# Folding the token numbers into the lower one-hots on VectorE, and moving the upper one-hots to GpSimd, in a two-layer attention kernel

## The chip, the core and the metric

The kernel runs on one core of a Trainium2 chip. The metric is the device time of one execution in microseconds (us). The core has five engines with instruction streams of their own: PE (TensorE, matrix products), DVE (VectorE), ACT (ScalarE), POOL (GpSimd) and SP, which here only starts DMAs. They meet through semaphores alone.

## The reference: what is computed

The layer takes x of shape 2 x 4096 x 256. An attention with 16 heads of width 16 ranks the queries of each head by a "sparsity" and lets only the best U = 307 of 4096 attend; the output rows of the others are zero before the last projection. A residual and a layer norm follow, then a feed-forward part (RWKV style) with a second residual and layer norm.

```python
scores = jnp.einsum('bhqd,bhkd->bhqk', q, k) * scale
sparsity = scores.max(axis=-1) - scores.mean(axis=-1)
_, top_idx = jax.lax.top_k(sparsity, U)
q_sel = jnp.take_along_axis(q, top_idx[..., None], axis=2)
scores_sel = jnp.einsum('bhud,bhkd->bhuk', q_sel, k) * scale
attn = jax.nn.softmax(scores_sel, axis=-1)
out_sel = jnp.einsum('bhuk,bhkd->bhud', attn, v)
out = jnp.zeros_like(q).at[bi, hi, top_idx].set(out_sel)
```

## The kernel before

**One plan for all engines.** `schedule()` writes one list of tokens, and every engine walks through it and issues its part of each token. So the order on an engine is that of the list, and a wait holds everything behind it on that engine.

**The main loop** has 2048 steps: 32 head-batches times 64 steps, two for each of the 32 query tiles. In a step PE makes the scores of 128 queries with half of the keys (`lead`, `second`, `main`: four products of 512 columns), ACT writes the absolute values of two of them to `AB` (L1033), and DVE takes the row maximum of `DP` + `AB` (L1189, 1024 elements a row). After the last step comes a tail: the rest of the attention and the feed-forward part of the second batch.

**Beside the main step** each step may take one step of `selection()` and one of `attention()` or, if that has nothing ready, of `background()` (projections and values, later the feed-forward part of the first batch). An attention step `st` is one product of 307 columns on PE, an exponential on ACT (L1068) and a subtraction on POOL (L1645); `pv` adds two products on PE.

**Selection** works on eight groups of heads, `GROUPS`: four of 5 heads (groups 0, 1, 4, 5) and four of 3 (groups 2, 3, 6, 7). It can start when the last head of its group has left the main loop, so group 7 is selected in the tail, with nothing of the main loop beside it. A search digit by digit finds the threshold (`parts`, `cmp`, `spread`, `cnt`, `digit`), `cut` to `rank2` give each chosen token its slot, and `slots` splits the slot number (0 to 306) into an upper part (slot // 16) and a lower part (slot % 16), which POOL copies to `fa` and `fb` as f16.

**The one-hots.** The list of chosen tokens comes from a product on PE (`idx`, L839) of two one-hot tables, summed over the 32 token tiles. `OB[:, j, :]` holds, for the lower value j (16 of them), the token's number where `fb` is j and zero elsewhere. `OA[:, :, j]` holds, for the upper value j (`A_COLS` = 20 of them), a one where `fa` is j. A row has 160 elements for 5 heads and 96 for 3. Before the change:

- `ob`: DVE compares `fb` with j (L1327, one operation for each j, two a step), and POOL multiplies the result by the token numbers `tokc` (L1593), behind a wait for each j.
- `oa`: DVE compares `fa` with two (in the tail four) numbers of a constant row `numbers` in one operation (L1332).
- In the main loop these take 8 + 10 = 18 steps of the plan with two values of j each; then 4 empty steps, then `idx`. In the tail they are 4 + 5 tokens with four values each.

**After the list** `ixdma` stores it, `gath` (POOL, indirect DMAs) fetches the chosen queries, and `attend` of the group may start, in turn.

Of the kernel before, what the change touches and what calls it, by code (L numbers as in the profile page):

```python
# [7 lines left out]
F16 = mybir.dt.float16  # L8
I32 = mybir.dt.int32
ALU = mybir.AluOpType  # L10
# [3 lines left out]
NT = L // 128  # L14
# [42 lines left out]
def schedule():  # L57
# [134 lines left out]
    def select(g):  # L192
# [30 lines left out]
        for j in range(0, 16, m):  # L223
            yield [("ob", g, j, m)]
        for j in range(0, A_COLS, m):
            yield [("oa", g, j, m)]
# [198 lines left out]
def attention_rwkv(nc, x, Wq, bq, Wk, bk, Wv, bv, Wo, bo, W_r, W_k, W_v, mu_r, mu_k, out):  # L425
    ctx = ExitStack()
    with ctx:
        def sb(name, shape, dt=F32):
            return ctx.enter_context(nc.sbuf_tensor(name, shape, dt))

        def sem(name):
            return ctx.enter_context(nc.semaphore(name))
# [33 lines left out]
        numbers = sb("numbers", [128, A_COLS], F16)  # L466
# [64 lines left out]
        def ff_tiles(count, w=D):  # L531
# [43 lines left out]
        sel_sl, sel_f, sel_ob, sel_tk, sel_oa, sel_ix = (sem(n) for n in (  # L575
            "sel_sl", "sel_f", "sel_ob", "sel_tk", "sel_oa", "sel_ix"))
# [66 lines left out]
        def _(pe):  # L643
# [189 lines left out]
            def idx(g, bank):  # L833
                n = GROUPS[g][2]
                o = claim(bank)
                pe.wait_ge(sel_tk, 16 * (g + 1))
                pe.wait_ge(sel_oa, A_COLS * (g + 1))
                for j in range(NT):
                    i = pe.matmul(o[0:n * A_COLS, 0:16 * n], OAf[:, n * A_COLS * j:n * A_COLS * (j + 1)],  # L839
                                  OB[:, :, n * j:n * j + n], start=j == 0, stop=j == NT - 1)  # L840
                i.then_inc(sel_pe, 1)
                owed[bank] = ((sel_ix, 2 * g + 1),)
# [292 lines left out]
        def _(dve):  # L1135
# [182 lines left out]
            def ob(g, j0, m):  # L1318
                n = GROUPS[g][2]
                if j0 == 0:  # L1320
                    if g == 0:
                        dve.wait_ge(*stored(46))
                        dve.wait_ge(*stored(47))
                        dve.wait_ge(qt_pe, 32)
                    dve.wait_ge(sel_f, g + 1)
                for j in range(j0, j0 + m):
                    dve.tensor_scalar(OB[:, j, 0:NT * n], fb[:, 0:NT * n], float(j), None, ALU.is_equal).then_inc(sel_ob, 1)  # L1327

            def oa(g, j0, m):
                w = NT * GROUPS[g][2]  # L1330
                dve.wait_ge(consts, 2)
                dve.tensor_tensor(OA[:, 0:w, j0:j0 + m], fa[:, 0:w].unsqueeze(2).broadcast_to([128, w, m]),  # L1332
                                  numbers[:, j0:j0 + m].unsqueeze(1).broadcast_to([128, w, m]),
                                  ALU.is_equal).then_inc(sel_oa, m)
# [101 lines left out]
            def f9(b, t, late):  # L1436
                if late:
# [7 lines left out]
                          spread=spread_, digit=digit, cut=cut, need=need_, rank1=rank1, rank2=rank2, slots=slots, ob=ob, oa=oa, idx=idx,  # L1445
# [6 lines left out]
        def _(pool):  # L1452
# [5 lines left out]
            def setup():  # L1458
# [12 lines left out]
                for n, sc in (("k", WS / 2), ("q", WS), ("v", WS)):  # L1471
# [7 lines left out]
                          allow_small_or_imprecise_dtypes=True)  # L1479
                pool.iota(numbers[:], pattern=[[1, A_COLS]], base=0, channel_multiplier=0,  # L1480
# [106 lines left out]
            def ob(g, j0, m):  # L1587
                n = GROUPS[g][2]
                tk = tokc[:].unsqueeze(2).broadcast_to([128, NT, n])
                for j in range(j0, j0 + m):  # L1590
                    v = OB[:, j, 0:NT * n].rearrange("p (t h) -> p t h", h=n)
                    pool.wait_ge(sel_ob, 16 * g + j + 1)
                    pool.tensor_tensor(v, v, tk, ALU.mult).then_inc(sel_tk, 1)  # L1593
# [164 lines left out]
            stages = dict(vset=vset, vev=vev, vones=vones, qzero=qzero, split=split, slots=slots, ob=ob, qgzero=qgzero, gath=gath, arr=arrange,  # L1758
# [157 lines left out]
```

## Time and profile before

| what | value |
|---|---|
| three timed runs | 3275.97, 3280.68, 3289.43 us (median 3280.68) |
| the profiled execution | 3272.47 us, of which the span is 3270.7 us |
| share of the span, PE, DVE, ACT, POOL | 91%, 90%, 87%, 48% |
| granted clock of PE | 0.982 of 2.4 GHz (mean) |
| L1189, the row maximum (DVE) | 2048 times, 2463.2 us busy |
| L1033, absolute values (ACT) | 4096 times, 2291.2 us busy |
| L1068 on `BP`, exponential (ACT) | 901 times, 429.5 us busy |
| L1645, subtraction (POOL) | 957 times, 665.3 us busy |

The profile lists instructions by line of the kernel, engine and tile. Durations overlap a little at their ends, so what an operation costs its engine is read as the distance from its start to the next start. A share of busy time is an average over stages with different limits.

### The profile page before, as it was taken

What the parts mean: (1) busy time and instruction counts of PE and PEld (TensorE: products, weight loads), DVE (VectorE), ACT (ScalarE), POOL (GpSimd) and SP (SyncE); (2) the same over time, 40 slices, a digit from 0 to 9 for tenths busy, and PEclk for the clock granted to TensorE, in tenths of its full rate; (3) what the DMA queues carried; (4) which work ended last, traced back from release to release, by engine and by line L of the source; (5) the groups of instructions that cost most, each with busy time, mean ns of one, the idle gap of its engine ahead of it and who ended that gap; (6) DMA issues with size and microseconds to landing.
All of it is one profiled execution on the core that took longest, in us unless ns stands there. A gap on an engine that the chain in (4) does not pass through costs nothing. (4 is left out here: it accounts for less than half of the span.)

```text
span 3270.7 us, 57975 instructions
## 1 busy us (share of the span) xinstructions
PE 2971.4 (91%) x15364; PEld 1361.9 (42%) x15364; DVE 2933.1 (90%) x5944; ACT 2836.0 (87%) x6246; POOL 1575.1 (48%) x2771
## 2 busy tenths in 40 slices
PE   6999899998989999998999999899999899997588
PEld 3333333333433443443343444444444343443477
DVE  4999999999999999999999999899999899998567
ACT  5999889997988999899899888799988699895466
POOL 3223122224644653654364564766455663557654
PEclk8999999999999999999999999999999999999889
DMA  6333323352151131123111244112141123202022
GB/s 188 85 101 109 81 72 84 86 25 40 37 38 27 35 41 26 23 40 34 32 36 36 51 52 44 37 34 41 37 52 37 30 38 28 41 15 16 15 83 73
DMA packets 263605, 163.58 MB, mean 50 GB/s; under 512 B 168876, under 2 KB 242796, under 8 KB 259180
## 3 DMA queue, kind: packets, MB, share of 16 engines
q1 hardware_dynamic: 255180, 156.41, 26.2%
q0 software_dynamic: 6144, 1.37, 0.5%
q8 instruction: 123, 2.02, 0.3%
q14 instruction: 206, 1.69, 0.2%
q10 hardware_dynamic: 1952, 2.10, 0.2%
HBM read 111.86 MB, written 47.86 MB: 49 GB/s over the span
## 5 line engine op out<-in xcount | busy, mean ns | idle before, releaser
L1189 DVE CUSTOM_DVE_ANT_0 JK<-DP,AB 128x1024 bf16<-128x1024 f32 x2048 | 2463.2, 1222 | 209.9 <-ACT AB L1033 76.1
L1033 ACT ACTIVATE AB<-CP 128x512 f32<-128x512 f32 x4096 | 2291.2, 622 | 203.5 <-PE CP L751 146.1
L770 PE MATMUL DP<-KS,QS 128*128 128x512 f16 x4096 | 1228.6, 382 | 65.2 <-DVE SPr L1189 54.2
L1645 POOL TENSOR_TENSOR SCR<-E 128x307 f16<-128x307 f32 x957 | 665.3, 709 | 510.3 <-ACT E L1068 505.7
L751 PE MATMUL CP<-KS,QS 128*128 128x512 f16 x2048 | 788.7, 385 | 53.9 <-ACT AB L1033 31.6
L760 PE MATMUL CP<-KS,QS 128*128 128x512 f16 x2048 | 789.4, 385 | 34.0
L770 PEld LDWEIGHTS DP<-KS,QS 128*128 128x128 f16 x4096 | 355.9, 99 | 366.2 <-DVE SPr L1189 183.1
L1068 ACT ACTIVATE E<-BP 128x307 f32<-128x307 f32 x901 | 429.5, 477 | 33.0 <-PE BP L860 29.6
L751 PEld LDWEIGHTS CP<-KS,QS 128*128 128x128 f16 x2048 | 197.3, 96 | 517.0 <-ACT AB L1033 451.3
L760 PEld LDWEIGHTS CP<-KS,QS 128*128 128x128 f16 x2048 | 196.7, 96 | 410.4 <-ACT AB L1033 374.4
L860 PE MATMUL BP<-QT,KA 128*128 128x307 f16 x901 | 266.4, 296 | 20.5 <-ACT QT L1060 19.0
L1456 POOL TENSOR_SCALAR SCR<-SCR 128x48 f16<-128x48 f16 (+2 forms) x122 | 50.2, 412 | 397.1 <-ACT SCR L1011 192.8
L1189 DVE DVE_READ_ACCUMULATOR2_ANT SPr<- 128x1 f32 x2048 | 168.9, 82 | 0.0
L875 PE MATMUL PV<-E,XT 128*128 128x307 bf16 x512 | 155.9, 305 | 9.1 <-POOL SCR L1645 7.7
L875 PE MATMUL PV<-E,VF 128*128 128x307 bf16 x512 | 153.3, 299 | 0.0
L876 PE MATMUL PV<-SCR,XT 128*128 128x307 f16 x512 | 151.9, 297 | 0.0
L876 PE MATMUL PV<-SCR,VF 128*128 128x307 f16 x512 | 149.7, 292 | 0.0
L860 PEld LDWEIGHTS BP<-QT,KA 128*128 128x128 f16 x901 | 88.1, 98 | 144.8 <-ACT E L1068 22.9
L1618 POOL DMA_INDIRECT SCR<-QN,idxs x96 | 100.4, 1046 | 59.1 <-DMA idxs<-IDX 31.7
L1658 POOL DMA_INDIRECT AO<-OG,idxs x96 | 100.7, 1049 | 33.4 <-issue 17.8
L1683 POOL TENSOR_SCALAR frs<-fmv 128x1 f32<-128x1 f32 x64 | 14.1, 220 | 144.0 <-DVE fmv L1377 143.6
L1654 POOL TENSOR_TENSOR OG<-OG,bvb 128x48 f32<-128x48 f32 x32 | 9.6, 299 | 144.9 <-DVE OG L1367 144.8
(405 smaller groups left out, 3138.2 us busy)
## 6 DMA issues: line engine op xcount, KB each, us to landing
KS<-KTC SPq DMA_DIRECT2D x256, 128.0 KB, 4.9
QS<-QSC SPq DMA_DIRECT2D x512, 64.0 KB
KA<-KTC SPq DMA_DIRECT2D x128, 128.0 KB, 3.9
QN<-SCR SPq DMA_DIRECT2D x16, 544.0 KB, 3.4
SCR<-in_L_attn_x SPq DMA_DIRECT2D x16, 512.0 KB, 5.0
AO<-E SPq DMA_DIRECT2D x16, 512.0 KB, 7.1
VF<-in_L_attn_x SPq DMA_DIRECT2D x64, 128.0 KB, 2.2
VF<-AO SPq DMA_DIRECT2D x64, 128.0 KB, 2.2
```

What stands on the lines that cost most here:

```text
L751: pe.matmul(o, qs, ks[0][:, 1, :], start=True, stop=True).then_inc(sc_c, 1)
L760: pe.matmul(o, qs, ks[1][:, 1, :], start=True, stop=True).then_inc(sc_c, 1)
L770: r = pe.matmul(o[:, 512 * j:512 * j + 512], qs, ks[j][:, 0, :], start=True, stop=True)
L860: pe.matmul(o[:, 0:U], KA[hx % 2][:, 128 * kc:128 * kc + 128], QT[hx % 2][:, 0:U], start=True, stop=True).then_inc(s_pe, 1)
L875: pe.matmul(PV[:, 0:U], v, EH[a % NE], start=kc == 0, stop=False)
L876: pe.matmul(PV[:, 0:U], v, EL[a % NE], start=False, stop=kc == NT - 1).then_inc(pv_pe, 1)
L1033: act.activation(AB[p % 3][:, 512 * j:512 * j + 512], BANK["C%d" % j], ACT.Abs).then_inc(ab_full, 1)
L1068: act.activation(E[a % NE][:], BANK[bank][:, 0:U], ACT.Exp, scale=2 * SCALE / (WS * WS)).then_inc(ex_act, 1)
L1189: dve.tensor_tensor_reduce(out=JK[p % 2][:], in0=BANK["D%d" % u], in1=AB[p % 3][:], scale=1.0, scalar=0.0, op0=ALU.add, op1=ALU.max, accum ...
L1618: pool.indirect_dma_start(out=QG[0:w, 3 * (hx % 8) + c, :], out_offset=None, in_=QNr[b], in_offset=bass.IndirectOffsetOnAxis(ap=ixf[0:w, k ...
L1645: pool.tensor_tensor(EL[a % NE], E[a % NE][:], EH[a % NE], ALU.subtract).then_inc(el_g, 1)
L1658: pool.indirect_dma_start(out=AOr[b], out_offset=bass.IndirectOffsetOnAxis(ap=ixf[0:w, k:k + 1], axis=0), in_=OG[i][0:w, c, :], in_offset= ...
```

## The change

DVE now makes the lower one-hots with their token numbers in one operation (compare with j, then multiply by `tokc`), so POOL's multiplication and its sixteen waits a group are gone. The comparison for the upper one-hots moves from DVE to POOL, one operation for each value instead of one for two or four, with one wait for `sel_f` a round. Both stand in the same ten rounds (five in the tail), and `numbers` is gone.

```diff
@@ select(g)
         m = 2 if gaps else 4
-        for j in range(0, 16, m):
-            yield [("ob", g, j, m)]
         for j in range(0, A_COLS, m):
-            yield [("oa", g, j, m)]
+            yield [("oa", g, j, m)] + ([("ob", g, j, m)] if j < 16 else [])
         for _ in range(4 * gaps):
             yield []
         yield [("idx", g, bank())]
@@ tensor
             def idx(g, bank):
-                pe.wait_ge(sel_tk, 16 * (g + 1))
+                pe.wait_ge(sel_ob, 16 * (g + 1))
                 pe.wait_ge(sel_oa, A_COLS * (g + 1))
@@ vector
+                tk = tokc[:].unsqueeze(2).broadcast_to([128, NT, n])
                 for j in range(j0, j0 + m):
-                    dve.tensor_scalar(OB[:, j, 0:NT * n], fb[:, 0:NT * n], float(j), None, ALU.is_equal).then_inc(sel_ob, 1)
-
-            def oa(g, j0, m):
-                w = NT * GROUPS[g][2]
-                dve.wait_ge(consts, 2)
-                dve.tensor_tensor(OA[:, 0:w, j0:j0 + m], fa[:, 0:w].unsqueeze(2).broadcast_to([128, w, m]),
-                                  numbers[:, j0:j0 + m].unsqueeze(1).broadcast_to([128, w, m]),
-                                  ALU.is_equal).then_inc(sel_oa, m)
+                    dve.scalar_tensor_tensor(out=OB[:, j, 0:NT * n].rearrange("p (t h) -> p t h", h=n),
+                                             in0=fb[:, 0:NT * n].rearrange("p (t h) -> p t h", h=n), scalar=float(j), in1=tk,
+                                             op0=ALU.is_equal, op1=ALU.mult).then_inc(sel_ob, 1)
@@ gpsimd
-            def ob(g, j0, m):
-                n = GROUPS[g][2]
-                tk = tokc[:].unsqueeze(2).broadcast_to([128, NT, n])
+            def oa(g, j0, m):
+                w = NT * GROUPS[g][2]
+                if g == 0 and j0 == 0:
+                    pool.wait_ge(*stored(46))
+                    pool.wait_ge(*stored(47))
+                    pool.wait_ge(qt_pe, 32)
+                pool.wait_ge(sel_f, g + 1)
                 for j in range(j0, j0 + m):
-                    v = OB[:, j, 0:NT * n].rearrange("p (t h) -> p t h", h=n)
-                    pool.wait_ge(sel_ob, 16 * g + j + 1)
-                    pool.tensor_tensor(v, v, tk, ALU.mult).then_inc(sel_tk, 1)
+                    pool.tensor_scalar(OA[:, 0:w, j], fa[:, 0:w], float(j), None, ALU.is_equal).then_inc(sel_oa, 1)
```

**DVE, the last lower round of group 0 and what follows**, before. ISA rows are the row maximum L1189 and the read of its accumulator; the rest are the one-hots.

```order
1195 L1327 TENSOR_SCALAR SCR<-fb 128x160 x2
1196 L1189 ISA JK,SPr<-DP,AB 128x1024
1197 L1189 ISA SPr 128x1
1198 L1332 TENSOR_TENSOR SCR<-fa,numbers 128x160x2
1199 L1189 ISA JK,SPr<-DP,AB 128x1024
1200 L1189 ISA SPr 128x1
1201 L1332 TENSOR_TENSOR SCR<-fa,numbers 128x160x2
```

The same rows of the changed kernel, where the row maximum has line L1186:

```order
1195 L1325 SCALAR_TENSOR_TENSOR SCR<-fb,tokc 128x160 x2
1196 L1186 ISA JK,SPr<-DP,AB 128x1024
1197 L1186 ISA SPr 128x1
1198 L1186 ISA JK,SPr<-DP,AB 128x1024
1199 L1186 ISA SPr 128x1
1200 L1186 ISA JK,SPr<-DP,AB 128x1024
1201 L1186 ISA SPr 128x1
```

The eight pairs stand at the same places in both, with another operation; the ten operations on `fa` that stood in the steps behind them are gone, and row maxima follow each other.

**POOL, the end of the one-hots of group 1**, before. L1645 is the subtraction of an attention step, L1654 and L1658 store a finished head.

```order
346 L1593 TENSOR_TENSOR SCR<-SCR,tokc 128x160 x2
347 L1645 TENSOR_TENSOR SCR<-E 128x307
348 L1593 TENSOR_TENSOR SCR<-SCR,tokc 128x160 x2
349 L1645 TENSOR_TENSOR SCR<-E 128x307
350 L1593 TENSOR_TENSOR SCR<-SCR,tokc 128x160 x2
351 L1645 TENSOR_TENSOR SCR<-E 128x307 x5
352 L1654 TENSOR_TENSOR OG<-OG,bvb 128x48
```

The same place in the changed kernel, where the subtraction has line L1638:

```order
346 L1586 TENSOR_SCALAR SCR<-fa 128x160 x2
347 L1638 TENSOR_TENSOR SCR<-E 128x307
348 L1586 TENSOR_SCALAR SCR<-fa 128x160 x2
349 L1638 TENSOR_TENSOR SCR<-E 128x307
350 L1586 TENSOR_SCALAR SCR<-fa 128x160 x2
351 L1638 TENSOR_TENSOR SCR<-E 128x307
352 L1586 TENSOR_SCALAR SCR<-fa 128x160 x2
353 L1638 TENSOR_TENSOR SCR<-E 128x307
354 L1586 TENSOR_SCALAR SCR<-fa 128x160 x2
```

POOL has a pair of operations beside each subtraction as before, now for ten steps instead of eight, and none of them waits for DVE in its round.

**ACT, where the main loop ends and the tail begins**, before: L1033 is the main step's, L1068 an attention step's, L1040 the start of the search of group 7.

```order
2657 L1068 ACTIVATE E<-BP 128x307
2658 L1033 ACTIVATE AB<-CP 128x512 x2
2659 L1068 ACTIVATE E<-BP 128x307
2660 L1040 COPY upper_half<-DP 72x512
2661 L1068 ACTIVATE E<-CP 128x307
2662 L1068 ACTIVATE E<-BP 128x307
```

The same place in the changed kernel (L1030, L1065 and L1037 are the same three):

```order
2672 L1065 ACTIVATE E<-BP 128x307
2673 L1030 ACTIVATE AB<-CP 128x512 x2
2674 L1065 ACTIVATE E<-BP 128x307
2675 L1037 COPY upper_half<-BP 72x512
2676 L1065 ACTIVATE E<-DP 128x307 x4
```

Selection takes 8 fewer steps in each group, so from group 3 on an attention may start 8 main steps earlier: 884 attention steps stand ahead of the tail instead of 876, and 140 instead of 148 in it.

## Rows read from the trace of the kernel before

**Rows 1.** The page, busy time of the engines (share of span, instructions).

```profile
PE 2971.4 (91%) x15364; PEld 1361.9 (42%) x15364; DVE 2933.1 (90%) x5944; ACT 2836.0 (87%) x6246; POOL 1575.1 (48%) x2771
```

**Rows 2.** Main steps with attention: busy time and count of L1189, maximum and accumulator read.

```profile
1120.50:1152.00 31.50, 29.36 (x48) 1.00 0.26 42
```

**Rows 3.** Timeline of DVE, group 0: start us, duration us, line, operation, tiles, count.

```profile
755.47 1.22 DVE L1189 CUSTOM_DVE_ANT_0 JK<-DP,AB 128x1024 bf16<-128x1024 f32 x1
...
756.61 0.31 DVE L1327 TENSOR_SCALAR SCR<-fb 128x160 f16<-128x160 f16 x2
756.83 1.22 DVE L1189 CUSTOM_DVE_ANT_0 JK<-DP,AB 128x1024 bf16<-128x1024 f32 x1
...
769.62 0.48 DVE L1332 TENSOR_TENSOR SCR<-fa,numbers 128x320 f16<-128x320 f16 x1
770.02 1.21 DVE L1189 CUSTOM_DVE_ANT_0 JK<-DP,AB 128x1024 bf16<-128x1024 f32 x1
```

**Rows 4.** Windows of 18 steps, groups 0 to 4, sum of seven: us, PE, PEld, DVE, ACT, POOL.

```profile
755.47:783.72 28.25, 22.94 (x112) 9.14 (x111) 28.25 (x65) 22.09 (x44) 13.49 (x28) 1.00 0.01 2
1038.28:1068.58 30.30, 25.81 (x127) 10.29 (x127) 30.23 (x67) 25.41 (x56) 20.66 (x35) 1.00 0.11 19
1315.47:1345.67 30.20, 26.47 (x129) 11.29 (x129) 29.55 (x62) 24.93 (x56) 22.72 (x45) 0.94 0.02 2
1593.60:1619.43 25.83, 21.95 (x96) 7.44 (x96) 25.76 (x66) 20.93 (x42) 10.67 (x23) 1.00 0.01 1
2046.68:2081.87 35.19, 27.96 (x123) 14.24 (x124) 32.16 (x74) 23.72 (x53) 27.66 (x62) 0.95 0.08 24
...
sum 210.24, PE 177.10 PEld 76.53 DVE 205.50 ACT 164.83 POOL 147.27; mean PE 25.30 PEld 10.93 DVE 29.36 ACT 23.55 POOL 21.04
```

**Rows 5.** Timeline of DVE and POOL, lower rounds of group 1, attention beside them.

```profile
1042.47 0.61 DVE L1327 TENSOR_SCALAR SCR<-fb 128x160 f16<-128x160 f16 x2
...
1044.14 0.61 DVE L1327 TENSOR_SCALAR SCR<-fb 128x160 f16<-128x160 f16 x2
...
1041.38 0.88 POOL L1593 TENSOR_TENSOR SCR<-SCR,tokc 128x160 f16<-128x160 f16 x2
1042.21 0.70 POOL L1645 TENSOR_TENSOR SCR<-E 128x307 f16<-128x307 f32 x1
```

**Rows 6.** Timeline of DVE and POOL, one lower round of group 2.

```profile
1322.48 3.53 DVE L1327 TENSOR_SCALAR SCR<-fb 128x96 f16<-128x96 f16 x2
...
1322.73 0.69 POOL L1645 TENSOR_TENSOR SCR<-E 128x307 f16<-128x307 f32 x1
...
1325.28 0.69 POOL L1645 TENSOR_TENSOR SCR<-E 128x307 f16<-128x307 f32 x1
```

**Rows 7.** Upper comparisons on DVE: count, min/median/max ns, first and last start, forms.

```profile
L1332 DVE TENSOR_TENSOR SCR<-fa,numbers x75: 342/481/1029, 768.1 to 3034.0; 128x320 f16<-128x320 f16 x40, 128x192 f16<-128x192 f16 x30, 128x384 f16<-128x384 f16 x5
```

**Rows 8.** Nearest rows for the new operations: DVE timeline, then POOL's copies to `fa`.

```profile
2045.12 0.42 DVE L1424 SCALAR_TENSOR_TENSOR VF<-VF,BP 128x256 f32<-128x256 f32 x1
2045.46 1.22 DVE L1189 CUSTOM_DVE_ANT_0 JK<-DP,AB 128x1024 bf16<-128x1024 f32 x1
...
L1456 POOL TENSOR_SCALAR fa<-upper_half x8: 273/300/327, 752.2 to 3028.5; 128x160 f16<-128x160 int32 x4, 128x96 f16<-128x96 int32 x4
```

**Rows 9.** Start of the tail, timeline of DVE and POOL.

```profile
2972.11 4.28 DVE L1216 TENSOR_SCALAR lower_half<-upper_half 72x512 int32<-72x512 int32 x1 [1.48 <-ACT upper_half L1040]
...
2972.14 4.81 POOL L1645 TENSOR_TENSOR SCR<-E 128x307 f16<-128x307 f32 x7
```

**Rows 10.** The chain that ended last, in the tail: start, us, what.

```profile
2972.11 4.29 DVE lower_half L1216
...
3029.33 2.35 POOL SCR L1593 x7
3031.76 4.39 POOL SCR L1593 x9
```

**Rows 11.** Timeline of DVE, upper comparisons of group 7 in the tail.

```profile
3031.51 3.20 DVE L1332 TENSOR_TENSOR SCR<-fa,numbers 128x384 f16<-128x384 f16 x5
```

More of the change, by code:

```diff
@@ L465, in attention_rwkv @@
         halfc = sb("halfc", [128, 1])
-        numbers = sb("numbers", [128, A_COLS], F16)
         xpart = sb("xpart", [128, 2, 8])
@@ L574, in attention_rwkv @@
             "sel_st", "sel_cmp", "sel_sp", "sel_pe", "sel_lim", "sel_key", "sel_m"))
-        sel_sl, sel_f, sel_ob, sel_tk, sel_oa, sel_ix = (sem(n) for n in (
-            "sel_sl", "sel_f", "sel_ob", "sel_tk", "sel_oa", "sel_ix"))
+        sel_sl, sel_f, sel_ob, sel_oa, sel_ix = (sem(n) for n in (
+            "sel_sl", "sel_f", "sel_ob", "sel_oa", "sel_ix"))
         arr, ah_pe, ah_act, s_pe, ex_act, el_g, el_d = (sem(n) for n in (
@@ L1444, in _ @@
             stages = dict(xtev=xtev, kbar=kbar, kev=kev, split=split, main=main, cap=capture, parts=parts, cmp=cmp,
-                          spread=spread_, digit=digit, cut=cut, need=need_, rank1=rank1, rank2=rank2, slots=slots, ob=ob, oa=oa, idx=idx,
+                          spread=spread_, digit=digit, cut=cut, need=need_, rank1=rank1, rank2=rank2, slots=slots, ob=ob, idx=idx,
                           st=st, otr=otr, f2=f2, f3=f3, f5=f5, f7=f7, f8=f8, f9=f9)
@@ L1478, in setup @@
                 pool.iota(tokc[:], pattern=[[128, NT]], base=-L // 2, channel_multiplier=1,
-                          allow_small_or_imprecise_dtypes=True)
-                pool.iota(numbers[:], pattern=[[1, A_COLS]], base=0, channel_multiplier=0,
                           allow_small_or_imprecise_dtypes=True)
@@ L1756, in f9 @@
                     pool.tensor_scalar(fo[k % 4], fo[k % 4], r[:, 0:1], r[:, 1:2], ALU.mult, ALU.add).then_inc(f_o3, 1)
-            stages = dict(vset=vset, vev=vev, vones=vones, qzero=qzero, split=split, slots=slots, ob=ob, qgzero=qgzero, gath=gath, arr=arrange,
+            stages = dict(vset=vset, vev=vev, vones=vones, qzero=qzero, split=split, slots=slots, oa=oa, qgzero=qgzero, gath=gath, arr=arrange,
                           st=st, put=put, f1=f1, f2m=f2m, f2r=f2r, f3=f3, f5=f5, f6k=f6k, f7=f7, f8=f8, f9=f9)
```

## The prediction, as it was put on record

> **What bounds the kernel now.** I read the page first: PE, DVE and ACT are all near nine tenths busy and POOL at half [rows 1]. With three engines that close, the mean says nothing on this change; what counts is which of them ends last in the 18 steps that hold the one-hots. So I looked at the pace of the main step. In steps with attention and without selection, 24 row maxima take 31.5 us, 1.31 a step [rows 2]. DVE alone needs less: from one row maximum to whatever stands behind it is 1.14 us [rows 3]. In a plain attention step DVE has slack of 0.17 us, and ACT and PE set the pace; with neither attention nor selection the pace is DVE's 1.14.
>
> With one-hots it turns round. The timeline of group 0 shows a lower pair adding 0.22 us (from its start at 756.61 to the next maximum) and an upper operation 0.40 us (769.62 to 770.02) [rows 3]: 1.36 and 1.54 us a step, both above 1.31. The windows of the 18 steps agree: DVE is busy 28.25 of 28.25 us in group 0 and 30.23 of 30.30 in group 1, where ACT has 25.41 [rows 4]. So here DVE sets the time and work taken from it is worth something, but only down to 1.31 where attention runs beside it.
>
> **DVE also waits for POOL there.** In group 1 the same lower pair lasts 0.61 instead of 0.31, and its round takes 1.67 (1042.47 to 1044.14): POOL's two multiplications and its subtraction run from 1041.38 to 1042.91, and DVE's pair gets through only behind them [rows 5]. In group 2 a pair lasts 3.53 us, while POOL works off subtractions and multiplications without a gap [rows 6]. The upper comparison, with two inputs in SBUF, is hit less: median 481 ns, longest 1029 [rows 7], so never by more than about one subtraction of POOL. I take from this that the operation with one input can be kept out by a whole backlog of POOL and that with two by about one operation at a time.
>
> **What is removed.** With undisturbed operations (a row of 96 elements instead of 160 costs about 0.19 and 0.27 instead of 0.22 and 0.40, by the comparison's minimum of 342 against 481 ns [rows 7] and the reduction's 1.14 us for 1024 elements), 18 steps are 8 x 1.36 + 10 x 1.54 = 26.3 us with 5 heads and 8 x 1.33 + 10 x 1.41 = 24.7 with 3. The seven windows in the main loop sum to 210.2 [rows 4]. Two of them, groups 4 and 5, hold the feed-forward part too, whose DVE work I put at 0.35 us a step, so 32.6 each. Undisturbed: 3 x 24.7 + 2 x 26.3 + 2 x 32.6 = 191.9. The other 18 us are waits, most of them the ones just shown: 5.5 in group 2 alone.
>
> **What is added on DVE.** The combined operation is not in the trace at this shape. The nearest row is one of the same kind with 256 elements: 0.34 us from start to start [rows 8]. At the reduction's 1.1 ns an element that is 0.24 us for 160 and 0.17 for 96. Bounds: 0.11 (half of the lower pair) and 0.34. I take 0.24 and 0.17, as the second input is a repeated token number and gives no reason for a faster form. A round is then 1.14 + 0.48 = 1.62, or 1.14 + 0.34 = 1.48.
>
> **What is added on POOL.** The nearest row for a comparison is the copy to `fa`, 273 to 327 ns [rows 8]; the bound above is half of a multiplication pair, 0.44 [rows 5]. With 0.28 a round costs POOL 0.56 and its subtraction about 0.66, 1.2 in all, below the round of DVE; even at 0.44 it is 1.5. So POOL does not become the bound. It is no longer led by DVE, so `sel_oa` could come late for `idx`, but there are two rounds and four empty steps behind DVE's last pair.
>
> **The ten rounds and eight freed steps.** Eight rounds with a pair, two without, and eight steps that now are plain ones. Group 0 (values beside it, 1.14): 8 x 1.62 + 10 x 1.14 = 24.4. Group 1: 8 x 1.62 + 10 x 1.31 = 26.1. Groups 2 and 6: 8 x 1.48 + 10 x 1.31 = 25.0. Group 3, where neither attention nor background has anything (25.83 us in its window, ACT 20.93 [rows 4]): 8 x 1.48 + 10 x 1.14 = 23.3. Groups 4 and 5, with 0.35 for the feed-forward part and about 1.5 in the others: 8 x 1.97 + 15 = 30.8. Sum 185.4 without waits. For waits I add 0.15 us to each of the 56 rounds, 8.4: less than the 0.30 a lower pair loses in group 1, more than the median upper comparison, which loses nothing. That makes 193.8, against 210.2: **-16.4**.
>
> **What moves.** The plan holds 884 attention steps before the tail instead of 876. They fill steps that ran at 1.14 and now run at 1.31: 8 x 0.17 = **+1.3**. In the tail the eight attention steps that are gone stood under the digit search of group 7, which sets its time by its own chain; I count nothing. Without that cover they would be worth 0.43 us each on ACT, 3.4.
>
> **The tail.** Two places of it lie on the chain [rows 10]. At 2972.11 DVE's first operation of the search lasts 4.28 us, because POOL has a backlog of seven subtractions [rows 9]; they queued behind the indirect DMAs of a `gath`. That `gath` now stands eight steps earlier, so much of the backlog will be gone, though `arr` now falls close to the same place: **-2.5**, between 0 and -3.8. Then POOL's 16 multiplications lie on the chain for 2.35 + 4.39 = 6.7 us. Twenty comparisons of 96 elements at about 0.25 are 5.0, plus what DVE's sixteen operations hold POOL up. In the tail the five upper comparisons took 0.64 each instead of the 0.47 that 384 elements need by rows 3 and the slope above, so neither engine shut the other out [rows 11]. I take **-1.3**, between -1.9 and +1.
>
> **Sum.** -16.4 + 1.3 - 2.5 - 1.3 = -18.9. Against the profiled execution (3272.5) that is 3253.6; this execution lies 8.2 below the median of the three timed runs, so against the median it is 3280.7 - 18.9 = 3261.8. I predict **3261 us**.
>
> **A rule that speaks against it.** DVE's new operation reads two tensors from SBUF while POOL reads SBUF beside it in every round. The page SBUF — State Buffer of the Trainium skill, section Who interferes with whom, says that a DVE instruction with two SBUF inputs contends with a GpSimd instruction that reads SBUF, and that whoever comes first keeps the shared ports for the whole instruction. By it the trace agrees for single upper comparisons (1029 ns against 481 [rows 7]); whether it costs time in each round no row tells. It is the third rival.
>
> **Rivals.**
> 1. *The stalls only move.* The large waits (5.5 us in group 2, the 4.28 in the tail) come from POOL's backlogs behind indirect DMAs; those stay, and another operation of DVE may be caught. Then only the undisturbed difference is left: 185.4 - 191.9 + 1.3 = -5.2, some 3275. For it speaks that the backlogs have a source that the change doesn't touch; against it, that the operation that was caught longest is replaced by a kind that never lost more than 0.55. Chance 0.33.
> 2. *No waits at all.* POOL no longer follows DVE's pair, and its work fits under the row maximum (1.2 against 1.14). Then the 8.4 go too: -27, 3253. Part of my forecast's range.
> 3. *Every pair waits.* If in the 40 rounds beside attention or feed-forward (groups 1, 2, 4, 5, 6) each of the two operations waits for a subtraction of 0.70, a round gains 1.4: 40 x 1.4 = 56, less the 6 counted, so +31, 3312. With one such wait a round it is +3, no change. It ends slower from about 1.0 us of wait a round. The tail's and group 2's upper comparisons speak against it: most lost nothing. Chance 0.07 for slower, 0.08 for about no change.
>
> Forecast, with a gain between 12 and 28 us: chance 0.52. A measurement of this kernel tells about 0.5% (16 us) from no change. Of the forecast's range about four fifths lie beyond that; with its edges and rival 1's luck on the good side I give faster 0.50, same 0.41, slower 0.09. The range for 8 in 10: from the cheap end (no waits, an operation near 0.11, about -40) cut to 3240, up to 3286, which holds rival 1 and the mild form of rival 3.
>
> **What would show it.** The combined operation near 315 ns for 160 elements and 250 for 96, with long ones below 1.0 us. No row maximum more than 1.7 us behind the one before in a quiet round of group 1; a value near 1.48 in groups 2 and 6. DVE busy some 35 us less in all, of which only half appears in the span, as ACT and PE hold the freed steps at 1.31. POOL's new operations near 0.28. The first search operation of the tail well below 4 us. I am wrong if DVE's operations last near 0.6 on average (rival 3), if POOL's comparison takes over 0.5 so that `idx` on PE waits for `sel_oa`, or if the rounds gain what is said but row maxima elsewhere lose it again (rival 1).

## The result, and the profile after

The changed kernel takes 3337.11 us (median of 4 runs, 3335.99 to 3338.69) against 3278.43 for the kernel before in the same session (4 runs): ratio 1.0174, 95% interval 1.0155 to 1.0192. It is slower by some 58 us. The forecast was 3261, with a range from 3240 to 3286 and a chance of 0.09 for slower.

The profiled execution has a span of 3336.9 us, 66.2 more than before. Its busy times, the line that answers to [rows 1]:

```profile
PE 2980.6 (89%) x15364; PEld 1370.3 (41%) x15364; DVE 2907.6 (87%) x5869; ACT 2833.1 (85%) x6246; POOL 1673.4 (50%) x2802
```

DVE did lose work (25.5 us of it, I had said some 35) and POOL gained 98. From the first row maximum to the last the time grew by 57.3 us, from 2907.67 to 2964.96; behind the last by 5.7; the other 3.2 lie ahead of the first maximum, where nothing of the selection runs.

The windows of 18 steps, as in [rows 4], show where. They begin with the last row maximum ahead of the one-hots. Here are groups 0, 1, 3 and 4 and the sum of all seven; columns are us, PE, PEld, DVE, ACT, POOL (busy and count), granted clock, DMA share, GB/s:

```profile
761.65:797.59 35.94, 24.99 (x142) 11.42 (x140) 26.20 (x57) 20.98 (x43) 28.77 (x32) 0.91 0.07 9
1049.53:1089.20 39.67, 27.68 (x151) 12.85 (x151) 26.98 (x59) 23.66 (x52) 34.56 (x37) 0.87 0.11 15
...
1617.10:1642.83 25.73, 22.98 (x127) 8.62 (x126) 24.90 (x60) 20.43 (x41) 19.80 (x27) 1.00 0.03 2
2074.38:2120.32 45.94, 30.59 (x150) 16.19 (x149) 28.32 (x64) 22.26 (x49) 41.46 (x64) 0.81 0.06 13
...
sum 266.63, PE 191.73 PEld 89.27 DVE 190.97 ACT 158.16 POOL 225.81; mean PE 27.39 PEld 12.75 DVE 27.28 ACT 22.59 POOL 32.26
```

210.24 us have become 266.63, +56.4 of the +57.3. In the slow windows DVE no longer fills the time (26.20 of 35.94, where [rows 4] had 28.25 of 28.25), and POOL's work in the seven went from 147.27 to 225.81. One thing makes the two sums unlike: with ten rounds in place of eighteen, `idx` now falls inside these windows and stood behind them before. Windows of 26 steps hold it in both kernels; they sum to 290.9 before and 351.7 after, +60.8. They still begin what stands behind `idx` (the list's store and `gath`) at another place in each. Windows of 60 steps hold that too, with 2879 products of PE before and 2899 after; they sum to 624.9 and 672.6, +47.7. Of the other 9.6 us of the main loop 3.0 lie ahead of the one-hots of group 0, where both kernels do the same work, so differences of a few us come with the single execution. I use both windows below.

The new operations, by line with min/median/max in ns, then POOL's by shape with count, busy time and mean, and idle time before:

```profile
L1586 POOL TENSOR_SCALAR SCR<-fa x160: 782/1045/1367, 761.3 to 3101.7; 128x160 f16<-128x160 f16 x80, 128x96 f16<-128x96 f16 x80
L1325 DVE SCALAR_TENSOR_TENSOR SCR<-fb,tokc x128: 242/312/1915, 762.8 to 3089.2; 128x160 f16<-128x160 f16 x64, 128x96 f16<-128x96 f16 x64
...
L1586 POOL TENSOR_SCALAR SCR<-fa 128x160 f16<-128x160 f16 x80 | 91.8, 1196 | 5.2
L1586 POOL TENSOR_SCALAR SCR<-fa 128x96 f16<-128x96 f16 x80 | 60.7, 800 | 5.2
```

The combined operation is as forecast (median 312 ns over both shapes, 315 and 250 foretold). POOL's comparison is not: 1196 ns on average for 160 elements and 800 for 96, where I had put 0.28 us for all. What that does is seen in group 1, on the timelines of DVE, of POOL and of PE (start us, us, engine, line, operation, tiles, shape, count, idle before and its releaser):

```profile
1056.16 0.55 DVE L1325 SCALAR_TENSOR_TENSOR SCR<-fb,tokc 128x160 f16<-128x160 f16 x2
1056.63 1.21 DVE L1186 CUSTOM_DVE_ANT_0 JK<-DP,AB 128x1024 bf16<-128x1024 f32 x1
...
1057.77 0.55 DVE L1325 SCALAR_TENSOR_TENSOR SCR<-fb,tokc 128x160 f16<-128x160 f16 x2
1058.24 1.21 DVE L1186 CUSTOM_DVE_ANT_0 JK<-DP,AB 128x1024 bf16<-128x1024 f32 x1
...
1060.86 2.46 POOL L1586 TENSOR_SCALAR SCR<-fa 128x160 f16<-128x160 f16 x2
1063.40 0.70 POOL L1638 TENSOR_TENSOR SCR<-E 128x307 f16<-128x307 f32 x1
1064.18 2.46 POOL L1586 TENSOR_SCALAR SCR<-fa 128x160 f16<-128x160 f16 x2
...
1077.44 2.44 POOL L1586 TENSOR_SCALAR SCR<-fa 128x160 f16<-128x160 f16 x2
...
1070.38 0.59 PE L767 MATMUL DP<-KS,QS 128*128 128x512 f16 x2
1080.03 2.97 PE L836 MATMUL BP<-SCR 128*100 128x80 f16 x32 [9.05 <-POOL SCR L1586]
```

DVE's round takes 1.61 us (1056.63 to 1058.24), just the 1.62 of the forecast. POOL's takes 3.32 (1060.86 to 1064.18): two comparisons and a subtraction. DVE starts its last pair at 1062.65, POOL ends its last at 1079.88. PE has come to `idx` by 1071 and stands there for 9.05 us, and behind it, in its queue, the scores of the next main steps: one single step of 12.81 us. Over the kernel this wait ends five times with POOL's comparison (idle time of PE just before L836, and of DVE before `own`):

```profile
issue: 45.0, 6
POOL SCR L1586: 42.7, 5
...
DVE own L1334: 42.9, 5
```

In groups 4 and 5 it is the feed-forward part's work on POOL that comes late, queued behind the comparisons. PE's waits for it (total, times, longest) sum to 23.8 us, against 11.9 before:

```profile
PE PV L895 <- POOL VF L1728: 12.3, 3, 6.9
...
PE PV L895 <- POOL VF L1718: 6.7, 3, 4.3
```

That is not the largest of them. ACT waits as well, for the small operation `fnm` of the feed-forward part that POOL does between its comparisons: 12.9 us at once in group 4 and 9.7 in group 5, against 5.1 and 2.8 at most before. The timelines of POOL, ACT and DVE in group 4:

```profile
2096.08 7.45 POOL L1586 TENSOR_SCALAR SCR<-fa 128x160 f16<-128x160 f16 x6
2103.64 0.55 POOL L1700 TENSOR_SCALAR VF<-VF,frs 128x256 f32<-128x256 f32 x1
2104.15 0.23 POOL L1660 TENSOR_SCALAR fnm<-fsum 128x1 f32<-128x1 f32 x1
...
2104.47 0.51 ACT L1085 ACTIVATE VF<-VF,fnm 128x256 bf16<-128x256 f32 x1 [12.90 <-POOL fnm L1660]
...
2106.17 1.23 DVE L1186 CUSTOM_DVE_ANT_0 JK<-DP,AB 128x1024 bf16<-128x1024 f32 x1 [13.06 <-ACT AB L1030]
```

The row maxima before and behind stand 14.28 us apart, the longest step of the main loop. PE waits 6.41 us of that for ACT, so a count of PE's waits for POOL leaves it out.

In the tail the search's first operation has lost its stall (4.28 in [rows 9]), though another one of the search, `spread` at 3051.24, now lasts 3.88 us, where none lasted over 0.50 before. The comparisons take 16.18 us in place of the 6.7 of [rows 10], and DVE, done with its sixteen operations in 3.16, waits 15.23:

```profile
3033.00 0.42 DVE L1213 TENSOR_SCALAR lower_half<-upper_half 72x512 int32<-72x512 int32 x1 [1.64 <-ACT upper_half L1037]
...
3086.30 3.16 DVE L1325 SCALAR_TENSOR_TENSOR SCR<-fb,tokc 128x96 f16<-128x96 f16 x16 [0.64 <-POOL fb L1449]
...
3104.69 0.20 DVE L1334 TENSOR_TENSOR own<-DP,ownh 60x48 f32<-60x48 f32 x1 [15.23 <-PE DP L836]
...
3086.35 16.18 POOL L1586 TENSOR_SCALAR SCR<-fa 128x96 f16<-128x96 f16 x20
```

### The profile page after: what moved, and what is told of

Its sections match the earlier page's. It is cut to its first block and busy times, and to the rows that moved or that the text cites. A ratio compares the mean times of both kernels' runs of the same rounds, so it can differ in the third digit from the quotient of the medians.

```text
span 3336.9 us, 57858 instructions
## 1 busy us (share of the span) xinstructions
PE 2980.6 (89%) x15364; PEld 1370.3 (41%) x15364; DVE 2907.6 (87%) x5869; ACT 2833.1 (85%) x6246; POOL 1673.4 (50%) x2802
## 5 line engine op out<-in xcount | busy, mean ns | idle before, releaser
L1186 DVE CUSTOM_DVE_ANT_0 JK<-DP,AB 128x1024 bf16<-128x1024 f32 x2048 | 2463.3, 1222 | 259.5 <-ACT AB L1030 95.8
L1030 ACT ACTIVATE AB<-CP 128x512 f32<-128x512 f32 x4096 | 2293.4, 623 | 249.8 <-PE CP L748 187.4
L1638 POOL TENSOR_TENSOR SCR<-E 128x307 f16<-128x307 f32 x957 | 665.0, 708 | 504.6 <-ACT E L1065 497.5
L1065 ACT ACTIVATE E<-BP 128x307 f32<-128x307 f32 x906 | 433.7, 479 | 29.9 <-PE BP L857 27.1
L1186 DVE DVE_READ_ACCUMULATOR2_ANT SPr<- 128x1 f32 x2048 | 169.3, 83 | 0.0
L1586 POOL TENSOR_SCALAR SCR<-fa 128x160 f16<-128x160 f16 (+1 forms) x160 | 152.5, 998 | 10.4
```

The lines of the kernel that those rows point to most:

```text
L1030: act.activation(AB[p % 3][:, 512 * j:512 * j + 512], BANK["C%d" % j], ACT.Abs).then_inc(ab_full, 1)
L1065: act.activation(E[a % NE][:], BANK[bank][:, 0:U], ACT.Exp, scale=2 * SCALE / (WS * WS)).then_inc(ex_act, 1)
L1186: dve.tensor_tensor_reduce(out=JK[p % 2][:], in0=BANK["D%d" % u], in1=AB[p % 3][:], scale=1.0, scalar=0.0, op0=ALU.add, op1=ALU.max, accum ...
L1586: pool.tensor_scalar(OA[:, 0:w, j], fa[:, 0:w], float(j), None, ALU.is_equal).then_inc(sel_oa, 1)
L1638: pool.tensor_tensor(EL[a % NE], E[a % NE][:], EH[a % NE], ALU.subtract).then_inc(el_g, 1)
```

## The experiments

**1. What the comparison costs by itself.** A small kernel of its own, POOL alone and nothing beside it, each form eight times in a row. It computes nothing of the reference. Four of its eleven forms:

```
pool.tensor_scalar(line[:, j, :], fa[:], 1.0, 0.0, ALU.mult, ALU.add)      # L37, dense
pool.tensor_scalar(comb[:, :, j], fa[:], 1.0, 0.0, ALU.mult, ALU.add)      # L41, every 20th element
pool.tensor_scalar(line[:, j, :], fa[:], float(j), None, ALU.is_equal)     # L45, dense
pool.tensor_scalar(comb[:, :, j], fa[:], float(j), None, ALU.is_equal)     # L49, every 20th element
```

> A program of its own that computes nothing of the reference: POOL alone runs eight operations each of ten forms on 160 (or 96) f16 elements, with no DVE beside it, so that each form's price stands by itself. Copy as multiply and add to a dense row; the same to every 20th element; comparison with a number to a dense row; the same to every 20th element; dense comparison of 96; comparison and multiply; multiply alone; comparison with f32 in and out; product of two tensors (POOL's operation before the change); strided comparison of 96; subtract and maximum. Theory A, the comparison itself is slow on POOL: dense and strided comparison both near 1.0 us for 160 elements and 0.75 for 96, the strided copy near 0.3. Theory B, the strided output is slow: dense comparison near 0.3, strided copy and strided comparison both near 1.0. Theory C, neither, DVE's operations beside it stretched it: all below 0.5 us.

By line, min/median/max in ns and the first and last start:

```profile
L37 POOL TENSOR_SCALAR line<-fa x8: 327/328/329, 3.0 to 5.0; 128x160 f16<-128x160 f16 x8
L41 POOL TENSOR_SCALAR comb<-fa x8: 889/1087/1087, 5.5 to 10.2; 128x160 f16<-128x160 f16 x8
L45 POOL TENSOR_SCALAR line<-fa x8: 607/612/624, 11.3 to 15.8; 128x160 f16<-128x160 f16 x8
L49 POOL TENSOR_SCALAR comb<-fa x8: 1173/1176/1228, 16.4 to 23.8; 128x160 f16<-128x160 f16 x8
```

A seventh of the distance from first to last start gives 0.29, 0.67, 0.64 and 1.06 us from start to start. Both causes are there: the comparison costs 0.35 more than the multiply and add of the copy I had taken as nearest row, and the output of every 20th element another 0.4. These are means. The first three of the eight strided comparisons follow each other at 0.79 us and the others at 1.24 to 1.29 (dense: 0.57 to 0.59, then 0.67 to 0.68), so from the fourth on the two together cost more than their sum. Multiplying by one with a single operation takes 611 ns too, so it isn't the comparing: the form with two operations, multiply then add, is the cheap one (comparison then multiplication takes 749). Even a dense comparison costs twice the row I priced it by. On this the Trainium skill (GPSIMD Engine Reference, section 3.1 Elementwise — side-by-side cycle accounting) keeps the rule "use DVE for elementwise"; the trace agrees, as DVE's combined operation has a median of 312 ns beside 1045 for POOL's comparison, on the same two row lengths.

**2. `idx` later.** The changed kernel with twelve more empty steps ahead of `idx`, so that POOL's backlog can run off.

```diff
-        for _ in range(4 * gaps):
+        for _ in range(16 * gaps):
             yield []
         yield [("idx", g, bank())]
```

> The changed kernel with 16 instead of 4 empty steps of the plan between the last one-hots and idx; everything is computed. Theory: the loss is PE waiting for POOL's comparisons at idx (single main steps of 7 to 13 us in six groups), and POOL's work itself is cheap while it is not waited for. Then 12 more steps of about 1.3 us (15 us) let POOL finish, those long steps shrink below 3 us, and the time is about 3337 minus 50, 3285 or less, though idx comes 4 steps later than before the change. Rival: POOL's occupation is the loss (its subtractions come late, pv on PE waits for them, DVE waits for the ports); then the long steps only move to other places and the time stays above 3315.

3347.47 us, ratio 1.0195 (1.0168 to 1.0221): no gain, so my theory, in which only PE's wait for the comparisons costs, fell as a full account. Where neither attention nor feed-forward stands beside, it was right in group 0. A window of 28 steps holds `idx` in every kernel (one of 26 doesn't hold it here): 39.12 us, against 47.66 with `idx` early and 41.45 in the kernel before. In group 3 it is 37.68, against 37.23 and 38.72. Over 60 steps, with what stands behind `idx`, group 0 takes 85.81 against 83.57 before and group 3 79.07 against 80.55, so that in sum nothing is left of the gain over before. Elsewhere POOL's subtractions of the attention come late instead, and PE waits for them (waits of PE; total, times, longest):

```profile
PE PV L872 <- POOL SCR L1638: 26.7, 16, 5.1
```

against 7.7 us, longest 3.1, for the same wait in the kernel before. Beside attention POOL needs 3.32 us for a round that DVE passes in 1.61, so POOL is the bound itself there, and moving who waits for it is worth nothing.

**3. The upper comparison back on DVE.** The changed kernel with its combined operation and ten rounds, but the upper comparisons as before:

```diff
-                    pool.tensor_scalar(OA[:, 0:w, j], fa[:, 0:w], float(j), None, ALU.is_equal)...
+                dve.tensor_tensor(OA[:, 0:w, j0:j0 + m], fa[:, 0:w].unsqueeze(2).broadcast_to([128, w, m]),
+                                  numbers[:, j0:j0 + m].unsqueeze(1).broadcast_to([128, w, m]), ALU.is_equal)...
```

> Only half of the change: the combined lower operation on DVE, but the upper comparison back on DVE as before (two values in one operation), both in the same ten rounds; POOL makes no one-hots at all. Theory, POOL's comparison is the whole loss: no waits of PE at idx, DVE's rounds are 1.14 + 0.48 + 0.40 = 2.02 us with 5 heads (8 of them) and 1.14 + 0.34 + 0.27 = 1.75 with 3, the eight freed steps run at 1.14 to 1.31; with the seven stretches at about 29 us each the time is that of before within 10 us, 3270 to 3285. Rival, something else in the merged rounds or in the moved attention steps costs time: 3300 or more also here.

3290.88 us, ratio 1.0015 (1.0 to 1.003). That is above the 3270 to 3285 I expected, but the kernel before ran at 3288.45 beside it. So there is no measurable change from before, and the +1.7% comes with POOL's comparison.

**4 to 7. POOL's operation made cheaper, nothing else.** All four take the index row from a table of constants, so that it no longer matters what POOL writes (the queries are then others than the reference selects); number 4 is that alone, the control. Number 5 has POOL write a dense copy by multiply and add, the price I had assumed; number 6 a dense comparison; number 7 the copy into every 20th element. In the cut below `dense` stands for the tile of `OA` read as one row for each value.

```diff
-                    pool.tensor_scalar(OA[:, 0:w, j], fa[:, 0:w], float(j), None, ALU.is_equal)
+                    pool.tensor_scalar(dense[:, j, 0:w], fa[:, 0:w], 1.0, 0.0, ALU.mult, ALU.add)   # 5
+                    pool.tensor_scalar(dense[:, j, 0:w], fa[:, 0:w], float(j), None, ALU.is_equal)  # 6
+                    pool.tensor_scalar(OA[:, 0:w, j], fa[:, 0:w], 1.0, 0.0, ALU.mult, ALU.add)      # 7
```

> A control. The changed kernel with all its operations, but the token list written to idw comes from a constant table (token number 16 times row plus column, times zero of the computed list), so the attention is computed for the wrong queries and what POOL writes to OA no longer matters. Every wait stays. All theories: within 5 us of the changed kernel (3337). If it is not, the table itself moves the time and the next three are read against this run.

> The control with POOL's comparison replaced by the cheapest form that the forms run showed (multiply and add, to a dense row: 0.29 us from start to start for 160 elements), the same count at the same places; the one-hots of the upper part are left out. This is the price that the prediction used. Theory, only POOL's price was wrong in the prediction: the stretches shrink to about 194 us in sum, no long step at idx, and the time is about 19 us below before, 3255 to 3268. Rival, the prediction was also wrong on the rest (two-input operations of DVE that wait for POOL in every round, moved attention steps): then it stays above 3275.

> The control with the comparison kept and only its output dense (one row for each value, which PE's product could not read as it stands; 0.64 us alone for 160 elements, 0.46 for 96). A round then costs POOL 1.3 + 0.7 = 2.0 us with attention beside it, above DVE's 1.62, 20 us over ten rounds with 5 heads, against about 21.5 us until idx. Theory, POOL's price times its count decides and idx waits only for what is left: about the time of before, 3265 to 3285. Rival, any comparison on POOL ruins it whatever its price: above 3310.

> The control with multiply and add instead of the comparison, the output strided as in the changed kernel (0.67 us from start to start alone for 160 elements). By price it equals the dense comparison, so the theory that only the sum of POOL's time counts expects the same time as that run within 6 us, 3265 to 3290. Rival, scattered two-byte writes cost something more beside DVE's operations (the records of the strided copy last 1.09 us though they follow each other at 0.67): 3300 or more.

Beside the runs above, with the sums of the seven windows. POOL's operation is given as its median duration and, for 160 elements, as the median from its start to the next start; the second is what it costs POOL:

| kernel | POOL's operation, duration, ns | start to start, us | 26 steps, us | 60 steps, us | ratio (95%) |
|---|---|---|---|---|---|
| before | | | 290.9 | 624.9 | 1 |
| after | 1045 | 1.26 | 351.7 | 672.6 | 1.0174 (1.0155 to 1.0192) |
| 4 control | as after | 1.26 | 352.3 | 673.3 | 1.0169 (1.0143 to 1.0196) |
| 7 copy, every 20th | 862 | 0.70 | 305.3 | 626.1 | 0.9999 (0.9986 to 1.0013) |
| 6 dense comparison | 574 | 0.69 | 306.5 | 627.5 | 1.0013 (1.0 to 1.0026) |
| 5 dense copy | 318 | 0.29 | 297.0 | 619.3 | 0.9978 (0.9966 to 0.999) |
| 3 none on POOL | | | 313.8 | 635.5 | 1.0015 (1.0 to 1.003) |

A window's sum comes from one execution, and the one of before lies 8 us under its median, so where sums are close the ratio decides. The control is where it should be. With the price alone changed, the loss goes. The rise isn't even: from 0.29 to 0.69 us some 0.3%, the same at 0.70, and at 1.26 it is 1.7%. Numbers 6 and 7 cost POOL the same in two different ways and end within 4.1 us of each other, so it is POOL's time that counts and not the comparing or the scattered output as such. (Number 6 took 3288.35 us, above the 3265 to 3285 of its expectation, beside 3284.84 for the kernel before.) That is how a wait behind a backlog behaves. By the group 1 timeline DVE and PE come to `idx` after 8 rounds of 1.62 and 6 plain steps of 1.31, 20.8 us. POOL's ten rounds take 30.6 in the changed kernel (1049.24 to 1079.88), but 21.3 in number 6 (1041.14 to 1062.41). In number 6 PE's wait for the comparison is nearly gone, but for the tail:

```profile
PE DP L837 <- POOL SCR L1590: 12.2, 1, 12.2
PE BP L837 <- POOL SCR L1590: 1.4, 1, 1.4
```

Number 5 is the one that tests the rest of my sum: with POOL at the price that I had assumed, it is faster, but by 0.1 to 0.34% (3 to 11 us), not by 18.9, so the rival of its expectation held. Its timeline shows one place where the rest went, DVE first, then POOL, in group 2:

```profile
1322.77 5.58 DVE L1326 SCALAR_TENSOR_TENSOR SCR<-fb,tokc 128x96 f16<-128x96 f16 x2
...
1321.64 1.10 POOL L1615 DMA_INDIRECT SCR<-QN,idxs  x1 [0.31 <-issue]
1322.76 0.71 POOL L1642 TENSOR_TENSOR SCR<-E 128x307 f16<-128x307 f32 x1
1323.42 0.52 POOL L1590 TENSOR_SCALAR SCR<-fa 128x96 f16<-128x96 f16 x2
1323.90 0.70 POOL L1642 TENSOR_TENSOR SCR<-E 128x307 f16<-128x307 f32 x1
...
1327.31 0.69 POOL L1642 TENSOR_TENSOR SCR<-E 128x307 f16<-128x307 f32 x1
```

POOL comes out of three indirect DMAs with work owed and does it, each operation started before the one ahead has ended, until 1328.5. DVE's combined operation, started at 1322.77, gets nowhere for 5.35 us: it has two inputs in SBUF and is shut out just as the lower pair of [rows 6] was. The same happens in group 6 (5.52 us at 2812.54). So a stall of 3.5 became one of 5.3.

**8. The ten rounds alone.** The kernel before, all its operations on their engines, in the ten merged rounds:

```diff
-        for j in range(0, 16, m):
-            yield [("ob", g, j, m)]
         for j in range(0, A_COLS, m):
-            yield [("oa", g, j, m)]
+            yield ([("ob", g, j, m)] if j < 16 else []) + [("oa", g, j, m)]
```

> Only the order of the rounds is changed: the kernel before with its own operations (lower comparisons on VectorE, multiplications on POOL, upper comparisons on VectorE), but lower and upper ones in the same ten rounds, so eight steps fewer a group. My theory: the order by itself is worth nothing, since VectorE has the same work in fewer steps and the freed steps are held at 1.31 us by ACT and PE: 8 x 1.76 + 2 x 1.54 + 8 x 1.31 = 27.6 us against 26.3 for 5 heads beside attention, 26.1 against 24.7 for 3 heads, no difference where no attention runs beside. Some +5 us in all, 0 to +12, ratio 1.000 to 1.004. Rival: the merged rounds put VectorE, the multiplications and POOL's subtractions closer together, and it is this that made the version with both one-hots on VectorE lose what the combined operation saved; then this one is slower by 15 us or more and row maxima stand over 2 us behind the one before.

3277.96 us (12 runs), ratio 0.9996 (0.9985 to 1.0006). The order by itself is worth nothing; my theory had at most a few us (ratio 1.000 to 1.004), and the rival, that merging costs 15 us, fell. A round on DVE's timeline takes 1.97 us (1041.52 to 1043.49):

```profile
1041.12 0.49 DVE L1330 TENSOR_TENSOR SCR<-fa,numbers 128x320 f16<-128x320 f16 x1
1041.52 1.22 DVE L1187 CUSTOM_DVE_ANT_0 JK<-DP,AB 128x1024 bf16<-128x1024 f32 x1
...
1042.66 0.51 DVE L1325 TENSOR_SCALAR SCR<-fb 128x160 f16<-128x160 f16 x2
1043.09 0.48 DVE L1330 TENSOR_TENSOR SCR<-fa,numbers 128x320 f16<-128x320 f16 x1
1043.49 1.21 DVE L1187 CUSTOM_DVE_ANT_0 JK<-DP,AB 128x1024 bf16<-128x1024 f32 x1
```

**9. The change only where it gained.** The changed scheme with `idx` 16 steps later in groups 0 and 3, the other groups as before, since number 2 had these two below the kernel before.

```diff
+        if g in (0, 3):
+            for j in range(0, A_COLS, m):
+                yield [("poa", g, j, m)] + ([("cob", g, j, m)] if j < 16 else [])
+            for _ in range(12 * gaps):
+                yield []
+        else:
             ...
```

> A candidate: the changed scheme (combined operation on VectorE, comparisons on POOL, ten rounds) only in groups 0 and 3, where no attention and no feed-forward stands beside it, with 16 empty steps before the index product there instead of 4; the other groups as in the kernel before. My theory (POOL is the bound only where it has subtractions too): group 0 gains some 4.7 us and group 3 some 2.8, as the windows of the run with the late index product showed for these two, so about -7 us, ratio 0.996 to 0.999, and no step there that waits for POOL's comparisons. Rival (gains in a group are given back elsewhere, as the waits move): 0.999 to 1.002.

3293.29 us, ratio 1.0042 (1.0026 to 1.0058): slower than before. Over 28 steps the two windows did gain, 2.4 and 1.0 us (39.08 and 37.70, against 41.45 and 38.72). The 4.7 and 2.8 that I expected were no gain to keep: they are what number 2 was ahead after 40 steps (52.85 against 57.59 in group 0), where the kernel before has already waited for its gathered queries and number 2 has that still to come. The gathered queries come later with `idx`, and PE waits longer for them some 19 us behind group 0's product, 3.04 us where it was 0.88:

```profile
811.85 0.37 PE L860 MATMUL CP<-identh,SCR 128*128 128x128 f16 x2 [3.04 <-POOL SCR L1673]
```

That step takes 6.06 us. Over 60 steps group 0 is at 84.75 (83.57 before) and group 3 at 78.98 (80.55), so here the rival (gained here, given back elsewhere) held, though the time lies above its 0.999 to 1.002 too. The profiled main loop is 13.0 us longer than that of before, and none of it has come by the end of group 3: counted from the first row maximum, the kernel is 0.7 us ahead of before at the end of that group's 60 steps. It all comes later, beside groups that the edit leaves as they were; in group 6, for one, two upper comparisons of DVE (two inputs in SBUF) last 1.64 and 2.83 us. What in the edit moves them there I did not find.

## Why the prediction was wrong

**The step that failed is a price.** "The nearest row for a comparison is the copy to `fa`, 273 to 327 ns", "With 0.28 a round costs POOL 0.56 and its subtraction about 0.66, 1.2 in all", and from it "So POOL does not become the bound". The copy is of another form (two operations, dense output). The comparison measured 1.26 us for 160 elements and 0.87 for 96 from start to start (mean durations 1.20 and 0.80), a round of POOL 3.32 in place of 1.2. My upper bound of 0.44 was no bound: it came from a multiplication with a dense output too. Before the change POOL had single scalar operations on one element alone (`fnm`, 0.25 us), which give no price per element, and none with an output of every 20th element. That should have opened the range upward, since the forecast turned on this price. The text named the consequence (over 0.5, and `idx` on PE waits for `sel_oa`), but gave it no chance.

**The term for the rounds, -16.4,** became +57.3 for the main loop. Its waits in the profiled execution: PE before `idx` for the comparisons, 24.7 us in groups 0, 1, 2 and 6 (the other 18.0 of the 42.7 are the tail's); in groups 4 and 5 the feed-forward part's operations on POOL, which stand behind the comparisons in its queue, 11.9 us more than before on PE and, by way of ACT's waits for `fnm`, 14.4 more over 26 steps (25.6 against 11.2; these overlap with PE's); and a slower PE. The granted clock is 0.87 and 0.81 in groups 1 and 4, where [rows 4] have 1.00 and 0.95: behind the 9.05 us of idle time it is 0.50 until 1086.1, and products of 512 columns last 0.63 us in place of 0.38. Over windows of 60 steps, which hold nearly the same products, PE's busy time grew from 562.1 to 572.7.

**What was right.** The combined operation (0.24 us start to start: 1.14 + 0.48 is the 1.61 measured). That ten merged rounds cost nothing by themselves (number 8). The term for the stall at the search's start, -2.5, came out in size: the search, from its first operation to the first one-hots, went from 56.9 to 53.3 us, -3.6. Its mechanism did so in part only, as the stall of 4.28 went to 0.42 and one of 3.88 on `spread` came. The tail's one-hots, -1.3, were mis-sized by the same price: +9.4 (6.7 to 16.18). The two rounds and four empty steps behind DVE's last pair were counted rightly in steps. Beside attention they are worth 7.9 us, and in group 1 POOL was done 16.7 us behind that pair (1079.88 against 1063.13).

**A second step was wrong, hidden behind the first.** "I take from this that the operation with one input can be kept out by a whole backlog of POOL and that with two by about one operation at a time", and in rival 1 the kind "that never lost more than 0.55". Number 5 shows 5.35 us for the operation with two, and the changed kernel itself one of 1.91 in group 6, while four operations of POOL ran. With POOL at the price that I assumed the kernel would have gained 3 to 11 us, which is what rival 1 said (-5.2), not the forecast's 18.9. The Trainium skill's rule (SBUF — State Buffer, section Who interferes with whom) has an operation of DVE with two inputs in SBUF contend with one of POOL that reads SBUF, and whoever comes first keep the shared ports for the whole instruction. The trace agrees that this kind is kept out, and shows a wait that lasted over thirteen of POOL's operations. The rival that I built on it (a loss of 0.70 at each operation) didn't come: in group 1, from 1054 on, POOL's comparisons follow each other with gaps of 0.07 to 0.08 us, and DVE's pairs beside them last 0.55 to 0.59.

## What to carry to other kernels

Price an operation by a row of the same form: same engine, same count of scalar operations, same step of the output; where there is none, the range must reach up by a factor, and if the verdict hangs on it, measure it alone first. When work is moved to a less busy engine, compare that engine's whole round with the time until the first consumer, not its share of the span: POOL at 48% had no room for a round of 3.3 us in one of 1.6. Empty steps ahead of the consumer cover a backlog only up to their own length. When windows of two plans are compared, see that the same work stands in both.

## What the runs showed of the hardware

- POOL's `tensor_scalar` for 160 float16 elements, from start to start: multiply and add, dense 0.29 us; one operation alone, multiplication 0.57, comparison 0.64. With an output of every 20th element (40 bytes apart) multiply and add 0.67, comparison 1.06 (number 1, means of eight). The durations that the profile gives are longer than that for the strided forms (1.09 for 0.67), so that the start of the next operation is what tells.
- In group 1 of the changed kernel the pair of comparisons at 1049.24 took 1.63 us to the next operation, those from 1054.22 on 2.54. Every group has this step, behind its third or fourth comparison (0.41 to 0.87 with 96 elements), and number 1 has it behind the third. Multiplication by one, eight times alike, doesn't have it (0.57 and 0.58). I have no explanation.
- A DVE operation with two inputs in SBUF (96 elements) lasted 5.35 us, where the shortest of its line lasts 0.24, while POOL worked without a gap, on thirteen operations that started in that time (number 5).
- In group 1 of the changed kernel PE's granted clock was 1.00 (2.4 GHz) until PE stood idle for 9.05 us, 0.50 (1.2 GHz) behind that from 1080.1 to 1086.1, and 1.00 again from 1086.3. Products of 512 columns lasted 0.61 to 0.63 us at the low level and 0.38 to 0.39 at the high one.
